# A graph network of two layers on one core: GpSimd's indirect transfers get more waits

## What is computed

```python
edge_index = jnp.stack([src, dst])
xn = _layernorm(x)
x = x + gnn0(xn, edge_index, edge_weight) + mix0(xn)      # segment_sum(support[col] * weight, row); linear attention
x = x + ffn0(_layernorm(x))                               # shared expert + 2 of 8 experts a node, 1024 wide
xn = _layernorm(x)
x = x + gnn1(xn, edge_index, edge_attr_2) + mix1(xn)      # messages of two directions, softmax over each node's edges
x = x + ffn1(_layernorm(x), router_edges)                 # 4 experts, gates from a graph attention over 32768 edges
```

## Time and profile before

| | us |
|---|---|
| median of three runs | 2920.31 |
| the profiled execution | 2916.22 |
| its span, first to last instruction | 2914.4 |
| TensorE busy | 2159.4 (74%) |
| GpSimd busy | 2021.0 (69%) |
| VectorE busy | 1680.6 (58%) |
| ScalarE busy | 1184.9 (41%) |
| TensorE's granted clock, mean share | 0.855 |

### The profile page before, as it was taken

One profiled execution on the slowest core, in us unless ns is written; L12 is line 12 of the kernel. 1 busy time (PEld: TensorE's weight loads), 2 busy tenths in 40 slices (PEclk: granted clock), 3 DMA queues, 4 the chain that ended last, 5 costly groups with the idle time before them and its releaser, 6 DMA issues. The chain is left out here.

```text
span 2914.4 us, 34544 instructions
## 1 busy us (share of the span) xinstructions
PE 2159.4 (74%) x9997; PEld 1671.4 (57%) x9997; DVE 1680.6 (58%) x4678; ACT 1184.9 (41%) x3151; POOL 2021.0 (69%) x2060
## 2 busy tenths in 40 slices
PE   0275482277666768999999997788877766899993
PEld 0055361144344437878888876455555545688883
DVE  8937889366679885110010026788887767333337
ACT  0111353155555542222222213799954444244442
POOL 4777777677777766777777633777777772777761
PEclk9996555588888887999999999899988876899996
DMA  2020000533333341366666633222222251211111
GB/s 65 2 63 2 6 3 2 193 105 105 106 105 102 103 96 37 118 176 196 199 191 193 194 104 103 51 54 53 54 51 52 53 47 9 55 36 35 18 19 46
DMA packets 173390, 233.34 MB, mean 80 GB/s; under 512 B 59819, under 2 KB 136622, under 8 KB 172206
## 3 DMA queue, kind: packets, MB, share of 16 engines
q0 software_dynamic: 73664, 103.00, 15.8%
q1 hardware_dynamic: 96888, 118.21, 13.1%
q10 hardware_dynamic: 2678, 10.29, 0.9%
HBM read 192.31 MB, written 39.04 MB: 79 GB/s over the span
## 5 line engine op out<-in xcount | busy, mean ns | idle before, releaser
L831 POOL DMA_INDIRECT slots_gnn<-rec_gnn,slot_row_gnn x782 | 770.6, 985 | 285.6 <-issue 229.6
L2359 POOL DMA_INDIRECT arena<-table,rec_gnn x440 | 456.0, 1036 | 162.0 <-issue 127.7
L1222 POOL DMA_INDIRECT rows_gnn<-support,xT x416 | 401.1, 964 | 132.6 <-issue 110.9
L1266 PE MATMUL banks<-rows_gnn,one_hot 128*128 128x256 f32 x832 | 301.0, 481 | 200.4 <-DMA rows_gnn<-support,xT 175.6
L1266 PEld LDWEIGHTS banks<-rows_gnn,one_hot 128*128 128x128 f32 x832 | 162.7, 227 | 319.6 <-DMA rows_gnn<-support,xT 180.4
L2931 POOL DMA_INDIRECT source_rows<-table_g,source_router x256 | 243.1, 950 | 78.0 <-issue 65.5
L2457 PE MATMUL banks<-weighted,one_hot 128*128 128x260 f32 x880 | 266.8, 456 | 2.6 <-DVE weighted L2554 1.9
L1871 ACT ACTIVATE hidden_private<-banks,b_private 128x256 f32<-128x256 f32 x256 | 107.3, 470 | 354.7 <-PE banks L1829 354.7
L1829 PE MATMUL banks<-slot_xT,w_private 128*128 128x256 f32 x1024 | 228.4, 381 | 1.7 <-DVE slot_xT L1885 1.7
L1841 PE MATMUL banks<-w_private,hidden_private 128*128 128x256 f32 x1024 | 226.1, 379 | 0.0
L2457 PEld LDWEIGHTS banks<-weighted,one_hot 128*128 128x128 f32 x880 | 186.9, 222 | 60.1 <-issue 26.7
(11 more groups left out here) (558 smaller groups left out, 3959.2 us busy)
## 6 DMA issues: line engine op xcount, KB each, us to landing
w_private<-in_w1p SPq DMA_DIRECT2D x32, 1024.0 KB
w_private<-in_w2p SPq DMA_DIRECT2D x32, 1024.0 KB
slots_gnn<-rec_gnn,slot_row_gnn POOLq DMA_INDIRECT x782, 2.1
slot_x<-zero_rows ACTq DMA_DIRECT2D x8, 1024.0 KB, 11.2
slot_rows<-slot_x SPq DMA_DIRECT2D x32, 256.0 KB, 7.4
slot_y<-slot_out SPq DMA_DIRECT2D x32, 256.0 KB, 2.2
arena<-table,rec_gnn POOLq DMA_INDIRECT x440
rows_gnn<-support,xT POOLq DMA_INDIRECT x416, 2.7
```

Of the source, the lines that this page charges most:

```text
L831: pool.indirect_dma_start(e.slots, bass.IndirectOffsetOnAxis(e.rows[:, j:j + 1], 0), e.rec[:, j, :], None)\
L1222: pool.indirect_dma_start(e.rows_in[:, k, :], None, table, bass.IndirectOffsetOnAxis(row, 0))\
L1266: mm = pe.matmul(bank_of(k // per), hot[:, k, :], e.rows_in[:, row, :], start=k % per == 0, stop=k % per == per - 1)
L2359: pool.indirect_dma_start(c.raw[:, t % RAW_RING, :], None, c.table1, bass.IndirectOffsetOnAxis(row, 0))\
```

## The change

Four things are added to GpSimd's stream, and one number is moved.

1. VectorE counts a new semaphore `vector_at` at 44 points of its four stages beside the first scatter, and `scatter_records` waits for the next count before the transfers listed in `BESIDE` (80, 83, ... 368).
2. The scatter of layer 1 uses a new function, `scatter_in_bursts`: one semaphore, and before every tenth transfer (`BURST`) a wait until all earlier ones have landed. The wait 16 transfers back goes. `send_nodes0` gets the same wait at every tenth send. `SCATTERED_FIRST` goes from 48 to 40.
3. `gather_messages` waits for TensorE's sums 28 tiles back (`AHEAD`) from tile 28 on, in place of 72 tiles back from tile 72 on.
4. The gathers of router rows also wait for TensorE's units, from row 24 on.

```diff
             equals(b - 2)
+            if b % 4 == 1:
+                dve.sem_inc(c.vector_at, 1)
...
-def scatter_records(c, block, ctx, e, begin=0, end=None):
-
-    end = e.per if end is None else end
+def scatter_in_bursts(c, block, ctx, e, begin, end):
+
+    turns = c.sem(ctx, f"scatter_turns_{e.name}_{begin}")
+    moved = c.sem(ctx, f"records_moved_{e.name}_{begin}")
+
+    @block.gpsimd
+    def _(pool):
+        pool.wait_ge(e.ranked, 1)
+        pool.wait_ge(e.filled, 16)
+        for j in range(begin, end):
+            if j > begin and (j - begin) % BURST == 0:
+                pool.wait_ge(moved, 16 * (j - begin))
+                pool.sem_inc(turns, 1)
+            pool.indirect_dma_start(e.slots, bass.IndirectOffsetOnAxis(e.rows[:, j:j + 1], 0), e.rec[:, j, :], None)\
+                .then_inc(moved, 16)
+        pool.wait_ge(moved, 16 * (end - begin))
...
+            if j in BESIDE:
+                pool.wait_ge(c.vector_at, BESIDE.index(j) + 1)
+                pool.sem_inc(turns, 1)
...
-SCATTERED_FIRST = 48
+SCATTERED_FIRST = 40
+BURST = 10
+BESIDE = (80, 83, 85, 88, 90) + tuple(102 + 16 * i // 5 for i in range(13)) + (155, 174, 190, 203)\
+    + tuple(234 + 34 * i // 7 for i in range(16)) + (333,) + tuple(344 + 6 * i for i in range(5))
...
+                j = t * CHOSEN + k
+                if j and j % BURST == 0:
+                    pool.wait_ge(sent, 16 * j)
+                    pool.sem_inc(turns, 1)
...
-                if t >= RAW_RING:
-                    pool.wait_ge(c.summed1, (t - RAW_RING) // HALF + 1)
+                if t >= AHEAD:
+                    pool.wait_ge(c.summed1, (t - AHEAD) // HALF + 1)
...
                 if j % HALF == 0 and turn:
                     pool.wait_ge(rows_in[h], 16 * HALF * turn)
+                    pool.sem_inc(turns, 1)
+                if j % HALF == 0 and j > FIRST_ROWS + HALF:
+                    pool.wait_ge(h_ready, FP * ((j - FIRST_ROWS) * 3 // 16))
                     pool.sem_inc(turns, 1)
...
-                    scatter_records(c, block, s, e1, 0, SCATTERED_FIRST)
+                    scatter_in_bursts(c, block, s, e1, 0, SCATTERED_FIRST)
                     send_nodes0(c, block, s)
-                    scatter_records(c, block, s, e1, SCATTERED_FIRST)
+                    scatter_in_bursts(c, block, s, e1, SCATTERED_FIRST, e1.per)
```

More of the change, by code:

```diff
@@ L729, in _ @@
             ch.then(dve.tensor_reduce(pos[:, lo:hi], found[:, 0:n, :], AX.X, ALU.add))
+            if g % 5 == 4:
+                dve.sem_inc(c.vector_at, 1)
         dve.wait_ge(within_made, batches)
@@ L810, in unpack, with scatter_records @@
         ch.then(dve.tensor_copy(self.e.idx[:], self.bank[:, 0:self.e.per]))
-def scatter_records(c, block, ctx, e, begin=0, end=None):
-    end = e.per if end is None else end
+def scatter_in_bursts(c, block, ctx, e, begin, end):
[12 more added lines that the diff above has]
+        pool.wait_ge(moved, 16 * (end - begin))
+def scatter_records(c, block, ctx, e):
+    begin, end = 0, e.per
     turns = c.sem(ctx, f"scatter_turns_{e.name}_{begin}")
@@ L912, in _ @@
                 residual(t - 1)
+            if t % 5 == 4:
+                dve.sem_inc(c.vector_at, 1)
         residual(T - 1)
@@ L1674 @@
 SHARED_FIRST = 3
-SCATTERED_FIRST = 48
+SCATTERED_FIRST = 40
+BURST = 10
+BESIDE = (80, 83, 85, 88, 90) + tuple(102 + 16 * i // 5 for i in range(13)) + (155, 174, 190, 203)\
+    + tuple(234 + 34 * i // 7 for i in range(16)) + (333,) + tuple(344 + 6 * i for i in range(5))
 def send_nodes0(c, block, ctx):
     sent = c.sem(ctx, "nodes_sent")
+    turns = c.sem(ctx, "node_turns")
     @block.gpsimd
@@ L1935 @@
 RAW_RING = 72
+AHEAD = 28
 ARENA = RAW_RING * 2 * MSG
@@ L2820 @@
 EARLY_TURN, EARLY_CARRY = 3, 6
+FIRST_ROWS = 16
 PARTS = 3
@@ L3431, in build @@
             with ExitStack() as s, nc.Block() as block:
+                c.vector_at = c.sem(s, "vector_engine_at")
                 scatter_records(c, block, s, e0)
```

## The result

On the chip of the prediction the changed kernel takes 2986.3 us in the median against 2923.0 us for the kernel before, measured beside it: 63 us more; the ratio of their times is 1.021, with a 95% interval of 1.017 to 1.025. 3003 us were predicted, from a median of 2920.3. Three of the changed kernel's four executions took 2981.8 to 2989.8 us and one 5350.4 us, of which there is no trace: the ratio leaves it out, the median has it in and is 2982.8 us without it.

What follows compares the result with a forecast made beforehand. Until 1710 us TensorE sets the time with GpSimd 49 us in hand; then late fetches delay everything. Fetches 88.8 us later, less 6.4 us back, give 82.4 us: 3003 us from a 2920.3 us median, range 2940 to 3035 us.

Steps and rivals of the forecast that it cites:

- The free waits: VectorE's points, the gathers' lead of 28 and TensorE's units before router rows: already satisfied when reached, cost 0.
- First scatter and sends: Second block's first 40 scatters and the sends: drains of 1.68 us and 10.5 us, last send at 1231.8 us.
- a private stage that starts later than 1246 us: Sign that the forecast is wrong: the private experts, expected not to move, start late.
- the cover: Last send lands at 1234.2 us, SyncE asks at 1242.90 us: 8.7 us left, so private experts don't move.
- The drains of the second scatter: 35 full waits among 351 transfers: 28 beside loads cost 107.2 us, 7 quiet ones 11.8 us.
- the landing beside the loads: Second scatter beside weight loads: mean landing taken as 4.25 us, making a drain of 3.83 us.
- rival B: Second scatter: bursts fall in step with loads, each drain there pays 6.48 us, kernel 3058 us; chance 0.05.
- What comes back: Last stage: 9.2 us of VectorE's waits go, less 2.8 us for TensorE's idle spell, net 6.4 us back.
- cold start: TensorE after some 75 us idle at the fetches: its first matmuls 2.8 us dearer, charged once.
- A: Second scatter: landings stay quiet, every drain costs 1.68 us, 58.8 us in all, kernel 2942 us; chance 0.12.
- C: Before the fetches: 49.2 us of slack hide all drains, time stays at 2920 us; chance 0.03.
- D: First scatter: points move transfers beside other VectorE work, up to 21 us back, drains hidden, 2899 us; chance 0.04.

Runs made afterwards that it cites:

- after_again: The whole changed kernel, run against the kernel before on a chip where that takes 4286 us: 3575 us, ratio 0.832.
- before_again: The kernel before, unchanged, with a profile of its own from a chip of the experiments: 4283 us against 4286, ratio 1.000.
- points_alone: Kernel before plus VectorE's points, the lead of 28 and TensorE's units before router rows, without drains: 3933 us against 4282, ratio 0.919.

## Why the prediction was right, and where it wasn't

All of this is the first chip.

**The free waits.** Right: VectorE's points, the lead of 28 and `FIRST_ROWS` show 0.3 us each. The first scatter ends at 552.9 us against 552.5.

**First scatter and sends.** The three drains cost 1.6 us each (forecast 1.68), the four of the sends 1.9, 4.6, 1.9 and 1.9 us, 10.4 together (forecast 10.5). But the sends began at 1164.95 us and not at 1159.2: `slot_to` came 6.2 us later than in the earlier trace rows. The stretch in which the router's matmuls start, in the kernel before:

```profile
1110.00:1120.00 10.00, 9.31 (x73) 9.07 (x72) 9.75 (x41) 5.24 (x12) 7.72 (x8) 0.84 0.03 3
```

and in the changed one:

```profile
1110.00:1120.00 10.00, 10.00 (x50) 10.00 (x49) 9.64 (x41) 4.42 (x10) 6.40 (x7) 0.50 0.03 3
```

TensorE's granted clock was at the lower of its two levels (1.2 GHz of 2.4) for all of it, where the kernel before still had part of it at the upper: 50 matmuls in place of 73. No step of the change is known to act there; it is taken as chance, which no run shows. By the prediction's own sign, "a private stage that starts later than 1246 us", this counts against it: SyncE asks at 1249.10 us. The cause isn't the one the sign was meant for. The last send is issued at 1239.1 us and the next scatter, which waits for its landing, at 1242.4, still 6.7 us before SyncE asks: the cover held. Second scatter: 7.4 us later than forecast, 5.8 us by the later sends and 1.6 us by their step (74.2 us from first to last in place of 72.6).

**The drains of the second scatter.** Here the forecast was off most. They cost 84.3 us and not 119.0, 2.4 us each and not 3.4. Of the 35, 25 cost 1.6 to 1.9 us, and ten cost 2.4 to 7.1. The term that was mis-sized is the landing beside the loads, and the sentence that failed is the one under rival B, that no burst length matches the experts' 14 us for long: a burst of ten with a quiet drain is 12.63 + 1.61 = 14.24 us against 14.25. That the two fit is an accident of this kernel's numbers. No run shows a burst that meets all phases of the full loads, so the 3.83 us of the forecast is untested as such; the 3.93 us of the burst of eight, which is in step as well, lies near it by luck. Of the ten dear ones, the first five steps have four (7.1, 4.7, 3.1, 3.0, until the step is found), five more follow the gaps behind the 113th and 226th transfer, which throw it out of step (5.1, 4.5, 3.3; 4.7, 5.3), and one of 2.4 stands alone. The way back can be followed: the last record ahead of the drains before the 120th, 130th, 140th and 150th transfer is issued 2.1, 5.6, 8.5 and 10.1 us after SyncE asked for a group's second matrix, the drains cost 5.1, 4.5, 3.3 and 1.8 us, and the place stays at 10.1 to 10.3 us up to the 180th. These gaps are the second miss, on the other side: 5.15, 6.39 and 2.96 us, of which 13.6 us are over the 0.30 that always stands there. The forecast had no term for them.

Together: -34.7 + 13.6 + 7.4 = -13.7 us, and the fetches started at 1785.1 us in place of 1799.0.

**What comes back.** From the first fetch to the first gather it is 96.2 us against 103.8 us: 7.5 us back, forecast 6.4. VectorE no longer waits for the shared expert, and TensorE pays for its cold start: 43 matmuls in 12.08 us, where 32 of the same took 7.17 us before its pause, are 2.5 us dearer (forecast 2.8). Its idle stretch was 59.4 us and not 75, since the rest of the shared expert runs first; nothing hangs on that.

**The sum.** 74.9 - 7.5 = 67.4 us at the first gather. Another 6.3 us came between there and the end (1106.8 against 1100.5 us), where the change has no step that binds; 5.2 of them in the gathers of layer 1, where a transfer takes 1045 ns in the mean against 1036 and one gap of 2.0 us stands. Two other executions of the changed kernel are 7 and 8 us faster than the profiled one, so it is put to scatter, not shown. 67.4 + 6.3 = 73.7 us on the profiled pair against 82.4 forecast. That the sum came this near is in part luck: drains 35 us too dear stand against 13.6 us of gaps, 7.4 us of lateness and these 6.3 us, which the forecast did not have.

**The rivals.** A (quiet landings, 2942 us) was wrong in its ground and half right in its price: most drains cost what it said. C and D fell: the fetches start 74.9 us behind the point to which the 49.2 us of cover reached. The case that decides elsewhere was not among them: that GpSimd's unbroken stream holds up other engines. The trace of before on the first chip shows nothing of it, with TensorE at 447.4 of 452 us beside the scatter. Rival D went in its direction, named VectorE only and gave it 21 us; on the chip of after_again all stages together give 711 us, and TensorE is held up as well as VectorE.

## What to carry to other kernels

A full wait on recent transfers costs a fixed quiet price (here 1.6 us for a record, 1.9 us for a row) or, as bursts of 8 and 10 had it, what is missing to the next round of a periodic load beside it: compare the burst's length with the load's period before taking a mean over phases. An engine with slack behind it can pay that, until the slack is used up (49 us here). And look at a long unbroken run of GpSimd's transfers on more than one chip: on all four chips of the experiments it held the other engines down, which no wait and no busy time in the first chip's profile gave away. Stops that cost 2% on the first chip gave back 17% on the one of these on which the same kernel was run.

## What the runs showed of the hardware

- While GpSimd issues indirect transfers step on step, 1.26 us each, TensorE starts one instruction per 1.40 us in before_again and points_alone, on two chips of the four; matmuls with a weight load between them are 2.8 us apart, some 2.1 or 3.5. GpSimd's own step grows little (1.335 us against 1.263 in the second scatter). Stops in which all has landed end it for a while: with one before every 8th transfer, mostly of 4 us, TensorE runs at full rate, with one before every 10th at 3.5 matmuls per us of 4.8, before every 13th at 1.3; stops of 0.65 us, with one transfer left in flight, give 0.60.
- A satisfied wait ahead of a transfer costs nothing that can be seen, for a landing ten transfers old or for another engine's point.
- In a scatter that drains and counts on one semaphore a stop of 3 us (to 8 us beside loads) stands behind every 113th transfer. With two semaphores 0.54 us are left of it with bursts of ten and 2.2 us with bursts of eight; without drains (two or four semaphores) there is none.
- Open: what the four chips have, or had at the time, that the first has not; whether the empty queue or the length of the stop frees the engines, and for how many transfers; where the 113 comes from.
